# SyncE's step in a different order: stack copies first, then the maxima's rows, the input two groups ahead, and the output's store last

## The reference

```
q = (x @ wq + bq), k = (x @ wk + bk), v = (x @ wv + bv)     8 heads of 16
scores = q . k / 4 ; attn = softmax(scores) ; o = attn . v
x1  = layernorm(x + o @ wo + bo, g1, be1)
out = layernorm(x1 + relu(x1 @ w1 + b1) @ w2 + b2, g2, be2)    hidden width 512
```

## Time and profile before

| | us |
|---|---|
| three executions | 4324.12, 4333.71, 4330.0 |
| median | 4330.0 |
| the profiled execution's own time | 4320.96 |
| its span, first to last instruction | 4318.9 |
| PE busy (share of the span) | 4177.6 (97%) |
| DVE busy | 3703.1 (86%) |
| POOL busy | 3615.5 (84%) |
| ACT busy | 3420.3 (79%) |
| chain that ended last: PE / SP's queue / issue | 39% / 24% / 11% |

### The profile page before, as it was taken

The page is one execution under the profiler, slowest core; times in us unless marked ns, Lnnn a source line. Parts: engine busy times, 40 slices in busy tenths (PEclk is TensorE's granted clock), DMA queues, the critical chain, the costliest instruction groups (busy, mean ns, idle before and its releaser), DMA issues.

```text
span 4318.9 us, 151819 instructions
## 1 busy us (share of the span) xinstructions
PE 4177.6 (97%) x50954; PEld 3637.0 (84%) x50954; DVE 3703.1 (86%) x9739; ACT 3420.3 (79%) x5889; POOL 3615.5 (84%) x4620
## 2 busy tenths in 40 slices
PE   5999999999999999999999999999999999999998
PEld 4888888888888888888888888888888888888886
DVE  6888888888888888888888888888888888888886
ACT  3888887877887887888888878888887887888886
POOL 5888888888888888888888878888888888888887
PEclk8999999999999999999999999999999999999999
DMA  5555555555555555555655555555555555565552
GB/s 128 146 146 146 149 146 148 148 140 145 149 143 150 144 149 146 142 147 150 150 148 148 146 140 149 146 148 147 147 148 139 148 148 148 146 151 146 149 149 58
DMA packets 1294637, 621.93 MB, mean 144 GB/s; under 512 B 636544, under 2 KB 1293696, under 8 KB 1293824
## 3 DMA queue, kind: packets, MB, share of 16 engines
q1 hardware_dynamic: 1293824, 611.80, 56.8%
HBM read 135.40 MB, written 67.11 MB: 47 GB/s over the span
## 4 chain that ended last, share of the span: by engine, by line
PE 39%; SPq 24%; issue 11%; POOL 10%; DVE 8%; DMA 5%; ACT 1%; DVEq 0%; POOLq 0%; ACTq 0%
SPq L252 14%; PE s_ps L680 6%; DMA stack<-parts 5%; PE oT_ps L707 5%; PE sT_ps L694 5%; PE bankC L645 5%; PE bankB L666 4%; SPq L246 4%; PE bankC L666 4%; SPq L209 4%; PE bankB L645 4%; PE bankA L720 3%; PE bankA L770 3%; POOL xT_parts L325 2%; POOL out_sb L336 2%
## 5 line engine op out<-in xcount | busy, mean ns | idle before, releaser
L404 ACT ACTIVATE prob_sb<-sT_ps 128x1024 f32<-128x1024 f32 x1024 | 1049.5, 1025 | 651.3 <-PE sT_ps L694 640.8
L510 DVE TENSOR_REDUCE max_sb<-s_ps 128x8 f32<-128x1024 f32 x1024 | 1214.3, 1186 | 13.3 <-PE s_ps L680 11.2
L277 POOL TENSOR_TENSOR parts<-rest_sb,parts 128x512 bf16<-128x512 f32 x512 | 585.8, 1166 | 251.7 <-ACT parts L378 251.7
L680 PEld LDWEIGHTS s_ps<-stack 96*128 96x128 bf16 x8192 | 463.2, 98 | 346.4 <-issue 290.0
L680 PE MATMUL s_ps<-stack 96*128 96x128 bf16 x8192 | 638.8, 221 | 84.5 <-DMA stack<-parts 55.2
L694 PE MATMUL sT_ps<-stack 99*128 99x128 bf16 x8192 | 628.6, 219 | 1.3 <-ACT prob_sb L404 1.3
L707 PE MATMUL oT_ps<-prob_sb,v_ones 128*32 128x128 f32 x16384 | 553.4, 276 | 3.4 <-ACT prob_sb L404 2.2
L666 PE MATMUL bankB<-w_sb,h_sb 128*128 128x128 f32 x4096 | 525.2, 281 | 2.3 <-ACT h_sb L385 2.3
L707 PEld LDWEIGHTS oT_ps<-prob_sb,v_ones 128*32 128x32 f32 x16384 | 416.1, 109 | 128.6 <-DVE max_parts L608 51.0
L694 PEld LDWEIGHTS sT_ps<-stack 99*128 99x128 bf16 x8192 | 504.0, 98 | 3.0 <-ACT prob_sb L404 1.8
L666 PE MATMUL bankC<-w_sb,h_sb 128*128 128x128 f32 x4096 | 499.2, 275 | 0.0
(11 more groups left out here) (78 smaller groups left out, 8720.8 us busy)
## 6 DMA issues: line engine op xcount, KB each, us to landing
stack<-parts SPq DMA_DIRECT2D x3072, 128.0 KB, 2.4
x_blocks<-in_x SPq DMA_DIRECT2D x1024, 64.0 KB, 2.8
x_sb<-in_x SPq DMA_DIRECT2D x256, 256.0 KB, 3.3
out<-out_sb SPq DMA_DIRECT2D x256, 256.0 KB, 2.4
stack<-max_parts SPq DMA_DIRECT2D x768, 8.0 KB, 2.2
w_sb<-in_L_conv_w SPq DMA_DIRECT2D x2, 256.0 KB, 3.1
be_row<-in_L_conv_ln_b SPq DMA_DIRECT2D x2, 64.0 KB, 5.3
g_row<-in_L_conv_ln_g SPq DMA_DIRECT2D x2, 64.0 KB, 5.6
```

What stands on the lines that cost most here:

```text
L277: pool.tensor_tensor(parts[:, r % 2, 3 * c + LO], rest_sb[:, c], parts[:, r % 2, 3 * c + MID], ALU.subtract).then_inc(lo_split, 1)
L404: act.activation(prob_sb[:, s % 2], sT_ps[:], ACT.Exp, scale=float(D) ** -0.5).then_inc(exp_done, 1)
L510: dve.reduce_max(max_sb[:, (r - lag) % 2, :, s], s_ps[:].rearrange("p (h k) -> p h k", h=H), AX.X).then_inc(max_done, 1)
L680: ins = pe.matmul(s_ps[:, h * P:(h + 1) * P], stack[0:PROD, (r - lag) % 4, 0, h, tok], stack[0:PROD, (r - lag) % 4, 1, h, tok], start=True ...
```

## The change

SP's step holds the same waits and DMAs, but for two things, in another order. First come the twelve stack copies of group r, then the three rows of the maxima of group r-2, then the block loads, now of group r+2 instead of r+1, then x of group r+1, and last the store of group r-7. The wait for `x_turned` now guards the block loads alone (group r+2 uses the buffer that group r has left), and the wait for `xb_done` is for group r-1, whose buffer x of group r+1 takes. Ahead of the loop the blocks of group 1 are loaded too.

```diff
+            load_blocks(1, 1)
             sp.dma_start(x_sb[:, 0], x_g[0]).then_inc(x_loaded[0], DMA)
 
             def step(t, r):
 
-                if live(t, r, 7):
-                    sp.wait_ge(out_ready, upto(t, r, 7, plus=1))
-                    sp.dma_start(out_g[t + (r - 7)], out_sb[:, (r - 7) % 2]).then_inc(out_stored[(r - 7) % 2], DMA)
-                if live(t, r, -1):
-                    if (v := upto(t, r, 0)) is not None:
-                        sp.wait_ge(x_turned, v)
-                    if (v := upto(t, r, 0)) is not None:
-                        sp.wait_ge(xb_done, v)
-                    sp.dma_start(x_sb[:, (r + 1) % 2], x_g[t + (r + 1)]).then_inc(x_loaded[(r + 1) % 2], DMA)
-                    load_blocks(t + (r + 1), r + 1)
+                if live(t, r, 0):
+                    for c, order in enumerate((Q_PARTS, K_PARTS)):
+                        sp.wait_ge(lo_split, upto(t, r, 0, per=2, plus=c + 1))
+                        for j, part in enumerate(order):
+                            sp.dma_start(stack[j:PROD:len(Q_PARTS), r % 4, c].rearrange("d h x -> d (h x)"),
+                                         parts[:, r % 2, 3 * c + part]).then_inc(stack_loaded[r % 2], DMA)
                 if live(t, r, 2):
                     sp.wait_ge(max_parts_made, upto(t, r, 2, plus=1))
                     for part in range(MAXROWS):
                         sp.dma_start(stack[PROD + part:PROD + part + 1, (r - 2) % 4, 0],
                                      max_parts[:, part]).then_inc(max_rows_loaded, DMA)
-                if live(t, r, 0):
-                    for c, order in enumerate((Q_PARTS, K_PARTS)):
-                        sp.wait_ge(lo_split, upto(t, r, 0, per=2, plus=c + 1))
-                        for j, part in enumerate(order):
-                            sp.dma_start(stack[j:PROD:len(Q_PARTS), r % 4, c].rearrange("d h x -> d (h x)"),
-                                         parts[:, r % 2, 3 * c + part]).then_inc(stack_loaded[r % 2], DMA)
+                if live(t, r, -2):
+                    sp.wait_ge(x_turned, upto(t, r, 0, plus=1))
+                    load_blocks(t + (r + 2), r + 2)
+                if live(t, r, -1):
+                    if (v := upto(t, r, 1, plus=1)) is not None:
+                        sp.wait_ge(xb_done, v)
+                    sp.dma_start(x_sb[:, (r + 1) % 2], x_g[t + (r + 1)]).then_inc(x_loaded[(r + 1) % 2], DMA)
+                if live(t, r, 7):
+                    sp.wait_ge(out_ready, upto(t, r, 7, plus=1))
+                    sp.dma_start(out_g[t + (r - 7)], out_sb[:, (r - 7) % 2]).then_inc(out_stored[(r - 7) % 2], DMA)
```

More of the change, by code:

```diff
@@ L253, in step @@
                                          parts[:, r % 2, 3 * c + part]).then_inc(stack_loaded[r % 2], DMA)
+                if live(t, r, 2):
+                    sp.wait_ge(max_parts_made, upto(t, r, 2, plus=1))
+                    for part in range(MAXROWS):
+                        sp.dma_start(stack[PROD + part:PROD + part + 1, (r - 2) % 4, 0],
+                                     max_parts[:, part]).then_inc(max_rows_loaded, DMA)
+                if live(t, r, -2):
[8 more added lines that the diff above has]
+                    sp.dma_start(out_g[t + (r - 7)], out_sb[:, (r - 7) % 2]).then_inc(out_stored[(r - 7) % 2], DMA)
             iterate(sp, step, 0, LEAD, LAST, 7)
```

## The result

The changed kernel takes 4945.0 us (median of 6 runs, 4930.27 to 4990.88) against 4325.24 us for the kernel before (6 runs). The ratio is 1.145, 95% interval 1.140 to 1.150: 620 us slower. The forecast was 4840 us with a range of 4670 to 4970. The profile shown is of an execution of 4970.16 us.

The account below looks back on a forecast made before the run. PE, 97% busy, was taken to bound the kernel at about 16.13 us a step. A loop of 12.27 + 6.3 = 18.57 us would replace the 16.52 us step, adding 252 x 2.05 = 517 us: 4840 us, range 4670 to 4970.

Parts of the forecast that it names:

- The ring: Low part, stack copies, maxima's rows, PE's quarter 2, projections, next low part: closes once a step, 18.57 us.
- The way forward: From the first low part's end through twelve copies and three rows to PE's start at quarter 2: 12.27 us.
- The way back: From PE's turned scores of quarter 2 to POOL's first low part's end: 6.3 us, ends 6.16 and 6.5.
- the sum made for it: Profiled execution of the kernel before plus the loss over 252 steps: 4320.96 + 517 = 4838 us.
- Rival D: PE's idle gap of about 2.4 us each step lowers the granted clock, one step in three: 5130 us, chance 0.07.
- A: The forecast case: maxima's rows late at PE's quarter 2, step 18.57 us, 4840 us, chance 0.82.
- The two stretches at the loop edge: Profile rows cited for the clock: PE busy 2.33 and 2.98 us of 5, clock 1.00, then 0.60 and 0.71.
- The 66.2 us of waits: PE's 101 quarter-3 scores waiting for the stack copies in the kernel before, taken as 66.2 us of PE's time.
- The two extremes, 17.3 and 19.5: Step length in us with all terms at their least or most: 4520 and 5070 us.
- What was to pay nothing: SP's block loads two groups ahead, x and the store last: expected to cost nothing, with over 5 and 8 us spare.
- The gain of the first part: Stack copies issued sooner, PE's waits for them gone: bounded by 66.2 us from waits, 99 us from the step's floor.
- Rivals B and C: B: rows in time, stack waits vanish, 4250 us, chance 0.07. C: lateness absorbed by PE's other waits, 4320 to 4340, 0.04.

Follow-up runs that it names:

- the gap filled: Changed kernel plus 24 dead matmuls of 96 rows on PE ahead of its wait for the maxima's rows: 4822.05 us, ratio to the kernel before 1.118.
- the rows-first kernel: Changed kernel with the three maxima's rows ahead of the twelve stack copies: 4282.71 us, ratio to the kernel before 0.991.

## Why the prediction was right, and where it was not

*The ring.* This was the step on which the forecast rested, and it held. That the maxima's rows behind the copies close a ring through PE's quarter 2, and that this outweighs the stack's earlier landing, was right: moved alone they give 1.140, put ahead they give 0.991.

*The way forward, 12.27 us.* Measured 12.03. The copies with their disturbances came to 8.40 (8.3 in the sum), the third row's issue to 1.42 instead of 1.35, SP's wake to 0.03 instead of 0.1, PE's start to 0.07 instead of 0.12, and the rows' landing to 2.03 instead of 2.3. The landing's median was 1.9 us behind the stack's copies and 2.2 right behind the input's loads. It isn't the input's loads as such: in the kernel with only the store moved the rows still follow them, with 2.1 us of idle SP between in the step shown, and the median is 1.9 too. The Trainium skill (DMA: Bandwidth & Descriptors, Anatomy of one DMA — SWDGE (gpsimd) path) has, for DMAs that GpSimd issues, about 2.0 us plus the bytes at 436 GB/s, from which 2.02 us is an estimate for 8 KB. SP issues the rows here: the mean of 2.03 agrees, the median of 1.9 and the mean of 2.23 with the gap filled do not.

*The way back, 6.3 us.* This is the term that was mis-sized: 7.04 measured. Its value at the high clock was right (6.22), but in half of the steps the clock fell. 0.74 us over 252 steps is 186 us; less 60 for the way forward that is 126, and the profiled execution is 4970 - 4838 = 132 us over the sum made for it. Filling the gap takes the clock's part away: the road back is shorter by 0.77 us, 194 us over 252 steps. The time fell by less, 123 us between the medians and 148 between the profiled executions, because the road forward was 0.17 us longer in that run, with the landing 0.20 us longer.

*Rival D.* I gave it 0.07 and 5130 us, as one step in three at 3.5 us. Its mechanism happened beside A's: one step in two, at 1.6 us on the ring. The prediction's own sign for D, a granted clock below 0.95, came up: 0.948 in the profiled execution, 0.943 to 0.952 over the six. I had ruled it out by one stretch in which PE was idle for 1.9 us and the clock stayed. In the kernel after 60 of the 90 gaps between 1.8 and 2.2 us were followed by a fall, so one stretch without a fall says little about a gap that comes in every step. The two stretches at the loop edge were no row for it either: they share one gap of 4.7 us, from 922.3 to 927.0. A and D were not alternatives; D's price belonged into A's sum with a weight.

*Luck.* The road forward was put too long by 60 us, and this hid a third of what the clock cost. Without it the same reasoning gives 4780 us, 165 us below 4945 and not 105. The time stands 25 us inside the range's upper end, and two of the six executions, 4970.16 and 4990.88, lie above it.

*Slips in the working.* The 66.2 us of waits add PE's 55.2 to 11.0 of its weight loads, and seven of the ten waits of these stand before scores that PE also waited for; PE itself lost 55.2. The 16.52 us is 16.51. The two extremes, 17.3 and 19.5, don't use all the ends listed: the wake's 0 and 0.5 are left out and the third row has 1.25 and 1.5 for 1.2 and 1.9. With the listed ends the sums are 17.2 and 20.3 us. None of this moves the forecast.

*What was to pay nothing.* Blocks, x and store in their new places paid nothing: of `x_sb`, `x_blocks` and `out_stored` only `x_sb` was waited for, once, for 0.6 us, and the rows-first kernel, which has all three, is faster than the kernel before. The gain of the first part, which I had bounded by 66 and 99 us, is 39 to 46 us where the rows don't stand in its way, and comes from the store's wait leaving the head of SP's step.

*Rivals B and C.* Neither occurred. PE's waits behind ACT and DVE did move along: POOL's wait for ACT's middle part grew from 251.7 to 903.9 us and hid nothing.

*Signs that I named* (measured in brackets). Step 18.5 us (19.07), PE's wait for the rows about 500 us (476.8), SP's wait for the low part some 3 us a step (4.8), PE's share near 87% (89), the clock near 0.99 (0.948: wrong).

## What to carry to other kernels

Order a queue's issues by how soon each is needed after it is ready, not by how much hangs on it: three 8 KB transfers behind twelve large ones cost 14%, though the queue had time to spare. When a transfer moves behind others, close the loop: from its landing through the engine that waits in order, back to what releases the transfers ahead of it; if that sum is over the present step, and no other loop is longer, it is the new step. A wait that blocks at the head of a queue's step can be worth moving to the end of the step (1.1% here), and a gap made on TensorE in every step is priced with the clock that may fall behind it.

## What the runs showed of the hardware that was not expected

- Work added made a kernel faster: 24 matmuls of 96 rows ahead of a wait took the mean granted clock from 0.948 to 0.990 and the time from 4945 to 4822 us. The same 24 on a TensorE without a gap cost 302 us.
- The granted clock fell behind idle gaps of TensorE as short as 1.6 to 2.2 us: in the kernel after behind 78 of 137 of them, and behind 1 of 62 shorter ones.
- 8 KB transfers landed 1.9 us after the start of their issue behind SBUF copies of 128 KB, 2.2 us right behind input loads, and 1.9 us behind input loads with some 2 us of idle SP between (medians).
